# One load per expert tile, and the second layer's weights split a tile earlier

## The chip, the cores and the metric

One core of a Trainium2 chip runs the whole program. The metric is the device time of one execution in microseconds; the median of 3 runs stands for a kernel.

## The reference

Two transformer layers are computed in float32 for 2048 tokens of 512 features. The first has linear attention with 32 heads, and beside it a mixture of 16 experts, of which a router gives each token two; the second has softmax attention and 64 low-rank adapters. The part that matters here is the experts:

```python
def step(y, p):
    w1, b1, w2, b2, w3, b3, ge = p
    h = jax.nn.silu(xt @ w1 + b1) * (xt @ w2 + b2)
    return (y + ge[:, None] * (h @ w3 + b3), None)
```

w1 and w2 are 512x128 and w3 is 128x512 per expert; ge is the token's weight for the expert, zero for all but two of the 16.

## The kernel before

Ahead of the experts the kernel runs the first layer's attention, the router and a shared expert; that is most of the span. The tokens are sorted by expert into 31 tiles of 256 slots (`NTILES`, `SLOT_T`); a tile belongs to one expert, and slots that hold no token are skipped by the gather. `routed_experts` computes the tiles; the results go to `y_slots` in DRAM, from which the second layer collects them.

Every matrix product in float32 is made of three passes over pairs of a rounded "high" part and a "low" rest: high by high, high by low, low by high (`three_passes`). So each operand is split first: ScalarE rounds it (`eh`, `exth`, `ehh`), and another engine subtracts to get the rest (`el`, `extl`, `ehl`).

The work of tile i, by engine, in a software pipeline:

- SP loads the expert's weights: `load12` brings w1, w2 and the two biases (513 KB) into `raw12`, `load3` brings w3 (256 KB) into `raw3`; it stores the tile's output (`y_tiles`, 512 KB) and loads a piece of the second layer's weights (`load_piece`, 116 KB).
- GpSimd copies the tile's token numbers (`indices`), gathers the token rows in two halves of 128 into `xin` (`gather`, two indirect DMAs), splits a piece of the second layer's weights, and makes the low part of w3 (line 2263).
- TensorE transposes the token rows into PSUM (`rows_transposed`, line 2117), multiplies by w1 and w2 (`inner`) and by w3 (`outputs`).
- ScalarE rounds the transposed rows (line 2161), w3 (line 2166), copies the biases (2170), rounds w1 and w2 (2172), rounds the layer-1 piece (2176), computes the activation (2180), rounds its product (2182) and copies half of the output (2187).
- VectorE makes the low part of the rows (2195) and of w1 and w2 (2201), the product of the two branches (2213), its low part (2216), and copies the other half of the output (2221).

Each engine runs one function `run(r, b)` per step, in a loop over r with b = 0 and 1. `tile(r, b, ahead)` gives the tile that stands `ahead` tiles before the one whose outputs are made in that step. So in one step TensorE transposes tile s+2, multiplies tile s+1 by w1 and w2, and makes the outputs of tile s. ScalarE rounds the rows, w1 and w2 of tile s+2, and w3 of tile s+1; GpSimd gathers tile s+4 and makes the low part of w3 of tile s+1. SP loads w1 and w2 of tile s+4 and w3 of tile s+3.

All buffers are pairs, used by even and odd tiles. Engines wait on counts: `pe_xt` says that a tile's rows are transposed (its `xin` is free), `pe_o` that an output half is made (w3's `eh` and `el` of that tile are free), `v_lo` and `p_lo3` that the low parts of w1, w2 and of w3 are made (the raw buffers are free). Each engine's instructions are carried out in the order in which they are written; a wait holds up all that stands behind it on that engine.

Of the kernel before, what the change touches and what calls it, by code (L numbers as in the profile page):

```python
# [8 lines left out]
F32 = mybir.dt.float32  # L9
F32R = mybir.dt.float32r  # L10
I32 = mybir.dt.int32
ALU = mybir.AluOpType
ACT = mybir.ActivationFunctionType
AX_X = mybir.AxisListType.X

P = 128
# [12 lines left out]
SEC = KC * P  # L29
# [1954 lines left out]
def routed_experts(nc, new_sem, at, ps, ex, l1_w, xn_dram, y_slots, ident, expert_of, token_at, table_in, w1h, w1l,  # L1984
# [12 lines left out]
    def pair(name, shape, dt=F32):  # L1997
        return [sb(f"{name}{i}", shape, dt) for i in range(2)]

    def sem(name):  # L2000
        return new_sem("e_" + name)

    W12 = 2 * SEC + 2
    raw12, raw3 = pair("eraw12", [P, W12]), pair("eraw3", [P, SEC])
    xin, cur = pair("exin", [P, 2, D]), pair("ecur", [P, 2], I32)

    bias = pair("ebias", [P, 2])
    eh = pair("eh", [P, 3 * SEC], F32R)
    el, xth, xtl = ([sb(f"{n}0", [P, c], F32R)] for n, c in (("el", 3 * SEC), ("exth", KC * SLOT_T), ("extl", KC * SLOT_T)))
    assert end <= blocks_end  # L2010
    for some, n, c in ((el, "el", 3 * SEC), (xth, "exth", KC * SLOT_T), (xtl, "extl", KC * SLOT_T)):
# [3 lines left out]
    s1, hf = pair("es", [P, SLOT_T]), pair("ehf", [P, SLOT_T])  # L2015
    hh, hl = pair("ehh", [P, SLOT_T], F32R), pair("ehl", [P, SLOT_T], F32R)
    yb = pair("ey", [P, 2, D])
    banks = [b[:].rearrange("p (k s) -> p k s", k=2) for b in ps[0:6]]
    xt, hp, op = [banks[0:2], banks[2:4]], banks[4:6], ps[6:8]
    dma_w, dma_w3, dma_x, dma_y, dma_l1 = ([sem(f"{n}{i}") for i in range(2)]  # L2020
                                           for n in ("dma_w", "dma_w3", "dma_x", "dma_y", "dma_l1"))
    a_l1, lo_l1 = sem("a_l1"), sem("lo_l1")
    pe_xt, pe_h, pe_o, a_hi, a_hi3, a_xh, a_s, a_hh, a_y, v_lo, v_xl, v_hf, v_hl, v_y, p_lo3, p_cur, p_clear = (
        sem(n) for n in ("pe_xt", "pe_h", "pe_o", "a_hi", "a_hi3", "a_xh", "a_s", "a_hh", "a_y", "v_lo", "v_xl",
                         "v_hf", "v_hl", "v_y", "p_lo3", "p_cur", "p_clear"))
    y_tiles = y_slots.rearrange("(p i s) d -> i p s d", p=P, s=2)
    def w(j):
        return slice(j * SEC, (j + 1) * SEC)
# [13 lines left out]
    def tile(r, b, ahead, n=NTILES):  # L2042

        r, b = r + (b + ahead) // 2, (b + ahead) % 2
        i = r * 2 + b
        return not isinstance(i, int) or 0 <= i < n, i, r, b

    def wait(eng, sem_, n):

        if not isinstance(n, int) or n > 0:  # L2050
            eng.wait_ge(sem_, n)

    def sync(sp):
        def expert(i):
            return sp.value_load(expert_of[0:1, bass.ds(i, 1)], min_val=0, max_val=E - 1)

        def load12(i, b):
            e = expert(i)
            wait(sp, v_lo, i * 2 - 2)
            sp.dma_start(raw12[b][:], ex[e, :, 0:W12]).then_inc(dma_w[b], 16)  # L2060

        def load3(i, b):
            e = expert(i)
            wait(sp, p_lo3, i - 1)
            sp.dma_start(raw3[b][:], ex[e, :, W12:W12 + SEC]).then_inc(dma_w3[b], 16)

        def load_piece(i, b):
            if isinstance(i, int) and i == 0:
                sp.wait_ge(pe_xt, 4)
            wait(sp, lo_l1, i - 1)  # L2070
            sp.dma_start(l1raw[b][:], l1_w[:, bass.ds(i * PIECE, PIECE)]).then_inc(dma_l1[b], 16)

        def lead():
            blocks_used(sp)
            load12(0, 0)
            load3(0, 0)

        def run(r, b):
            is_tile, i, _, n = tile(r, b, 4)
            if is_tile:  # L2080
                load12(i, n)
            is_tile, i, _, n = tile(r, b, 3)
            if is_tile:
                load3(i, n)
            is_tile, i, _, n = tile(r, b, 0)
            if isinstance(i, int) and i == NTILES - LATE:

                for k in range(LATE):
                    c = slice(k * LATE_COLS, (k + 1) * LATE_COLS)
                    sp.dma_start(w1_late[:, c], l1_w[:, L_CUT + c.start:L_CUT + c.stop]).then_inc(dma_l1[0], 16)  # L2090
            if is_tile:
                sp.wait_ge(a_y, i + 1)
                sp.wait_ge(v_y, i + 1)
                sp.dma_start(y_tiles[i], yb[n][:]).then_inc(dma_y[n], 16)
            is_piece, i, _, n = tile(r, b, 2, PIECES)
            if is_piece:
                load_piece(i, n)

        def rest():
            load12(1, 1)  # L2100
            run(-1, 0)
            all_steps(sp, run)

        return lead, rest

    def tensor(pe):
# [47 lines left out]
    def scalar(a):  # L2154
        def run(r, b):
            is_tile, i, half, n = tile(r, b, 2)
            if is_tile:
                wait(a, pe_h, i - 1)
                for h in range(2):
                    a.wait_ge(pe_xt, i * 2 + h + 1)  # L2160
                    a.copy(xth[n][:, 2 * h:2 * h + 2, :], xt[n][h][:]).then_inc(a_xh, 1)  # L2161
            is_3, i3, half3, n3 = tile(r, b, 1)
            if is_3:
                wait(a, pe_o, i3 * 2 - 2)
                a.wait_ge(dma_w3[n3], half3 * 16 + 16)
                a.copy(eh[n3][:, w(2)], raw3[n3][:]).then_inc(a_hi3, 1)  # L2166
            if is_tile:
                a.wait_ge(dma_w[n], half * 16 + 16)
                wait(a, v_hf, i - 1)
                a.copy(bias[n][:], raw12[n][:, 2 * SEC:W12])  # L2170
                for j in range(2):
                    a.copy(eh[n][:, w(j)], raw12[n][:, w(j)]).then_inc(a_hi, 1)  # L2172
            is_piece, k, half_k, nk = tile(r, b, 0, PIECES)
            if is_piece:
                a.wait_ge(dma_l1[nk], half_k * 16 + 16)
                a.copy(w1h[:, bass.ds(k * PIECE, PIECE)], l1raw[nk][:]).then_inc(a_l1, 1)
            if is_3:
                a.wait_ge(pe_h, i3 + 1)
                wait(a, v_hf, i3 - 1)
                a.activation(s1[n3][:], hp[n3][:, 0, :], ACT.Silu, bias=bias[n3][:, 0:1]).then_inc(a_s, 1)  # L2180
                a.wait_ge(v_hf, i3 + 1)
                a.copy(hh[n3][:], hf[n3][:]).then_inc(a_hh, 1)
            is_tile, i, half, n = tile(r, b, 0)
            if is_tile:
                a.wait_ge(pe_o, i * 2 + 1)
                wait(a, dma_y[n], half * 16)
                a.copy(yb[n][:, 0, :], op[0][:]).then_inc(a_y, 1)

        return lambda: run(-1, 0), lambda: all_steps(a, run)

    def vector(v):
# [33 lines left out]
    def gpsimd(pool):  # L2225
        def indices(i, n):

            pool.wait_ge(table_in, 1)
            pool.tensor_copy(cur[n][:], token_at[:, bass.ds(i * 2, 2)]).then_inc(p_cur, 1)
            pool.wait_ge(p_cur, i + 1)  # L2230

        def gather(n):
            for s in range(2):
                pool.indirect_dma_start(xin[n][:, s, :], None, xn_dram,
                                        bass.IndirectOffsetOnAxis(ap=cur[n][:, s:s + 1], axis=0),
                                        bounds_check=T - 1, oob_is_err=False).then_inc(dma_x[n], 16)

        def lead():
            blocks_used(pool)
            for b in range(2):  # L2240
                pool.memset(xin[b][:], 0.0).then_inc(p_clear, 1)
            pool.wait_ge(p_clear, 2)
            for b in range(2):
                indices(b, b)
                gather(b)

        def run(r, b):
            is_tile, i, half, n = tile(r, b, 4)
            if is_tile:
                wait(pool, dma_x[n], half * 32)  # L2250
                indices(i, n)
                pool.wait_ge(pe_xt, i * 2 - 2)
            is_piece, k, _, nk = tile(r, b, -1, PIECES)
            if is_piece:
                c = bass.ds(k * PIECE, PIECE)
                pool.wait_ge(a_l1, k + 1)
                pool.tensor_tensor(w1l[:, c], l1raw[nk][:], w1h[:, c].bitcast(F32), ALU.subtract).then_inc(lo_l1, 1)
            if is_tile:
                gather(n)
            is_3, i3, _, n3 = tile(r, b, 1)  # L2260
            if is_3:
                pool.wait_ge(a_hi3, i3 + 1)
                pool.tensor_tensor(el[n3][:, w(2)], raw3[n3][:], eh[n3][:, w(2)].bitcast(F32),
                                   ALU.subtract).then_inc(p_lo3, 1)

        return lead, lambda: run(-1, 0), lambda: all_steps(pool, run)

    return {"sync": sync, "tensor": tensor, "scalar": scalar, "vector": vector, "gpsimd": gpsimd,
# [568 lines left out]
```

## Time and profile before

| what | us |
|---|---|
| median of 3 runs (2571.44 to 2572.82) | 2572.6 |
| the profiled execution | 2570.18 |
| its span | 2568.3 |
| TensorE busy in the span | 2495.5 |
| GpSimd busy | 1508.9 |
| VectorE busy | 1172.4 |
| ScalarE busy | 1152.2 |

Busy time of TensorE counts matmuls whose ends are modelled, so a busy TensorE need not be at its peak. The experts' stretch is about 180 us of the span, from 2066 to 2250 us. In rows of the trace, PE is TensorE, PEld its weight loads, DVE VectorE, ACT ScalarE, POOL GpSimd and SP the engine that issues loads and stores. `out<-in` names the tile written and those read, and what stands in square brackets is the idle time of the engine just before, with what ended it.

### The profile page before, as it was taken

What the parts mean: (1) busy time and instruction counts of PE and PEld (TensorE: products, weight loads), DVE (VectorE), ACT (ScalarE), POOL (GpSimd) and SP (SyncE); (2) the same over time, 40 slices, a digit from 0 to 9 for tenths busy, and PEclk for the clock granted to TensorE, in tenths of its full rate; (3) what the DMA queues carried; (4) which work ended last, traced back from release to release, by engine and by line L of the source; (5) the groups of instructions that cost most, each with busy time, mean ns of one, the idle gap of its engine ahead of it and who ended that gap; (6) DMA issues with size and microseconds to landing.
All of it is one profiled execution on the core that took longest, in us unless ns stands there. A gap on an engine that the chain in (4) does not pass through costs nothing.

```text
span 2568.3 us, 39435 instructions
## 1 busy us (share of the span) xinstructions
PE 2495.5 (97%) x13338; PEld 2140.1 (83%) x13338; DVE 1172.4 (46%) x1937; ACT 1152.2 (45%) x2182; POOL 1508.9 (59%) x1523
## 2 busy tenths in 40 slices
PE   7999999999999999999999999999999999969999
PEld 6888888888888888778888888888888888857777
DVE  6333333434343435763334343434343588865443
ACT  5444444444444444443444444444444457733332
POOL 5756656666575754765666766757575578731210
PEclk9999999999999999999999999999999999979999
DMA  4211110111111112211111011111111178931100
GB/s 166 87 48 40 55 63 31 63 47 61 36 58 47 56 40 99 94 48 48 40 55 63 31 63 47 59 35 61 47 56 40 60 245 305 301 101 34 37 29 33
DMA packets 84950, 188.00 MB, mean 73 GB/s; under 512 B 12610, under 2 KB 30674, under 8 KB 84870
## 3 DMA queue, kind: packets, MB, share of 16 engines
q1 hardware_dynamic: 76326, 170.13, 20.0%
q0 software_dynamic: 8544, 16.82, 2.2%
q8 instruction: 48, 0.79, 0.1%
q14 instruction: 32, 0.26, 0.0%
HBM read 168.00 MB, written 26.79 MB: 76 GB/s over the span
## 4 chain that ended last, share of the span: by engine, by line
PE 85%; DVE 7%; ACT 4%; issue 2%; DMA 1%; POOL 1%; ACTq 0%; SPq 0%; DVEq 0%
PE bank L95 24%; PE bank L96 23%; PE bank L97 23%; PE bank L1081 4%; PE bank L1064 4%; PE bank L1082 2%; PE bank L1065 2%; DVE el L2201 2%; ACT exth L2161 1%; ACT eh L2172 1%; ACT eh L2166 1%; DVE ehf L2213 0%; DMA l_stage<-y_slots,slot_of 0%; POOL l_stage L2720 0%; PE bank L539 0%
## 5 line engine op out<-in xcount | busy, mean ns | idle before, releaser
L1805 POOL TENSOR_TENSOR wl<-w_in,wh 128x512 fp32r<-128x512 f32 x510 | 587.7, 1179 | 189.5 <-ACT wh L1348 183.2
L95 PE MATMUL bank<-xh,wh 128*128 128x512 f32 x1400 | 560.7, 400 | 0.7 <-ACT bank L1296 0.7
L97 PE MATMUL bank<-xh,wl 128*128 128x512 f32 x1400 | 546.6, 390 | 0.0
L1823 POOL TENSOR_TENSOR sqacc<-sqacc,sq 128x512 f32<-128x512 f32 x128 | 165.6, 1294 | 379.3 <-ACT sq L1333 368.2
L1348 ACT CAST wh<-w_in 128x512 fp32r<-128x512 f32 x502 | 263.6, 567 | 274.0 <-POOL w_in L498 274.0
L96 PE MATMUL bank<-xl_sums,wh 128*128 128x512 f32 x800 | 315.8, 395 | 0.0
L97 PEld LDWEIGHTS bank<-xh,wl 128*128 128x128 f32 x1400 | 263.0, 188 | 57.3
L95 PEld LDWEIGHTS bank<-xh,wh 128*128 128x128 f32 x1400 | 263.5, 188 | 53.4 <-ACT bank L1296 0.9
L1602 DVE TENSOR_TENSOR acc<-bank,acc 128x512 f32<-128x512 f32 x240 | 165.7, 691 | 299.6 <-PE bank L97 299.6
L95 PE MATMUL bank<-wh,xh 128*128 128x256 f32 x912 | 260.3, 285 | 3.3 <-DVE xl L550 3.3
L96 PE MATMUL bank<-wl,xh 128*128 128x256 f32 x912 | 258.4, 283 | 0.0
L96 PE MATMUL bank<-xl,wh 128*128 128x512 f32 x600 | 234.6, 391 | 0.0
L1559 DVE TENSOR_TENSOR ms<-bank,dcur 128x384 f32<-128x384 f32 x256 | 142.3, 557 | 154.4 <-PE bank L1065 145.2
L95 PE MATMUL bank<-oh,yh 128*128 128x512 f32 x512 | 200.7, 392 | 6.7 <-DVE acc L1600 5.3
L1577 DVE SCALAR_TENSOR_TENSOR yf<-gT,bank 128x512 f32<-128x512 f32 x128 | 88.0, 687 | 249.1 <-PE bank L1082 249.1
L96 PE MATMUL bank<-ol,yh 128*128 128x512 f32 x512 | 200.0, 391 | 0.0
L97 PE MATMUL bank<-oh,yl 128*128 128x512 f32 x512 | 199.8, 390 | 0.0
L1582 DVE SCALAR_TENSOR_TENSOR yl<-yf,little,yh 128x512 fp32r<-128x512 f32 x128 | 131.0, 1023 | 137.0 <-ACT yh L1338 134.8
L1565 DVE TENSOR_TENSOR bank<-bank,t 128x512 f32<-128x512 f32 x128 | 89.5, 699 | 195.3 <-PE bank L97 183.5
L95 PEld LDWEIGHTS bank<-wh,xh 128*128 128x128 f32 x912 | 174.5, 191 | 4.9 <-DVE xl L550 2.1
L96 PEld LDWEIGHTS bank<-xl_sums,wh 128*128 128x128 f32 x800 | 150.6, 188 | 29.6
L96 PEld LDWEIGHTS bank<-wl,xh 128*128 128x128 f32 x912 | 174.5, 191 | 0.7
(354 smaller groups left out, 5394.4 us busy)
## 6 DMA issues: line engine op xcount, KB each, us to landing
w_in<-in_w_pairs_dram SPq DMA_DIRECT2D x100, 512.0 KB, 3.8
o_in<-in_o_pairs_dram SPq DMA_DIRECT2D x32, 512.0 KB, 4.8
eraw<-in_ex_dram SPq DMA_DIRECT2D x31, 513.0 KB, 5.1
y_slots<-ey SPq DMA_DIRECT2D x31, 512.0 KB, 6.0
w_in<-in_w_pairs_dram SPq DMA_DIRECT2D x56, 256.0 KB, 3.1
dcur<-in_decay_dram SPq DMA_DIRECT2D x32, 384.0 KB, 3.0
eraw<-in_ex_dram SPq DMA_DIRECT2D x31, 256.0 KB, 5.1
out_dram<-acc SPq DMA_DIRECT2D x16, 256.0 KB, 2.0
```

Of the source, the lines that this page charges most:

```text
L95: pe.matmul(out, wh, mh, start=start and i == 0, stop=False, skip_group_check=True)
L96: pe.matmul(out, wh, ml, start=False, stop=False, skip_group_check=True)
L97: ins = pe.matmul(out, wl, mh, start=False, stop=stop and i == n - 1, skip_group_check=True)
L1064: pe.matmul(sc[i % 2][:, 0:S], kT[:, hd, s0:s0 + P], qT[:, hd, s0:s0 + S], start=True, stop=True)
L1081: pe.matmul(out, v0, ms[i % 2][:, 0:S], start=True, stop=False, skip_group_check=True)
L1348: a.copy(wh[:, cols], w_in[:, cols]).then_inc(w_hi, 1)
L1559: v.tensor_tensor(ms[i % 2][:], sc[i % 2][:, 0:MC], dcur[:, ITEMS[i][0], :], ALU.mult).then_inc(v_mask, 1)
L1565: v.tensor_tensor(pj[2][:], pj[1][:], t5[:], ALU.add).then_inc(v_c, 1)
L1582: v.scalar_tensor_tensor(yl[g % 2][:], yf[:], nwcur[:, g % 2:g % 2 + 1], yh[g % 2][:].bitcast(F32), ALU.mult, ALU.subtract).then_inc(v_yl, 1)
L1602: v.tensor_tensor(now[:, t, :], op[t % 2][:], now[:, t, :], ALU.add).then_inc(v_acc, 1)
L1805: pool.tensor_tensor(wl[:, cols], w_in[:, cols], wh[:, cols].bitcast(F32), ALU.subtract).then_inc(w_lo, 1)
L1823: pool.tensor_tensor(sqacc[:, c], sqacc[:, c], sq[:], ALU.add).then_inc(p_sq, 1)
```

## The change

The two raw buffers become one of 1538 columns, with views `raw12` and `raw3` of it, and one load fills it. It waits for `p_lo3` alone. ScalarE rounds w3 of tile s+2 where it rounded that of tile s+1, and does it after the activation. GpSimd makes the low part of w3 of tile s+2 in a function `low3`, which also waits for `v_lo` of the same tile (so that `p_lo3` stands for the whole raw buffer), and which stands ahead of the gather in the step.

```diff
-    raw12, raw3 = pair("eraw12", [P, W12]), pair("eraw3", [P, SEC])
+    raw = pair("eraw", [P, W12 + SEC])
+    raw12, raw3 = [x[:, 0:W12] for x in raw], [x[:, W12:W12 + SEC] for x in raw]
...
-        def load12(i, b):
-            e = expert(i)
-            wait(sp, v_lo, i * 2 - 2)
-            sp.dma_start(raw12[b][:], ex[e, :, 0:W12]).then_inc(dma_w[b], 16)
-
-        def load3(i, b):
+        def load(i, b):
+
             e = expert(i)
             wait(sp, p_lo3, i - 1)
-            sp.dma_start(raw3[b][:], ex[e, :, W12:W12 + SEC]).then_inc(dma_w3[b], 16)
+            sp.dma_start(raw[b][:], ex[e]).then_inc(dma_w[b], 16)
...
             is_tile, i, _, n = tile(r, b, 4)
             if is_tile:
-                load12(i, n)
-            is_tile, i, _, n = tile(r, b, 3)
-            if is_tile:
-                load3(i, n)
+                load(i, n)
...
-            is_3, i3, half3, n3 = tile(r, b, 1)
-            if is_3:
-                wait(a, pe_o, i3 * 2 - 2)
-                a.wait_ge(dma_w3[n3], half3 * 16 + 16)
-                a.copy(eh[n3][:, w(2)], raw3[n3][:]).then_inc(a_hi3, 1)
...
+            is_1, i1, _, n1 = tile(r, b, 1)
+            if is_1:
+                a.wait_ge(pe_h, i1 + 1)
+                wait(a, v_hf, i1 - 1)
+                a.activation(s1[n1][:], hp[n1][:, 0, :], ACT.Silu, bias=bias[n1][:, 0:1]).then_inc(a_s, 1)
+            if is_tile:
+
+                wait(a, pe_o, i * 2 - 2)
+                a.copy(eh[n][:, w(2)], raw3[n]).then_inc(a_hi3, 1)
+            if is_1:
+                a.wait_ge(v_hf, i1 + 1)
+                a.copy(hh[n1][:], hf[n1][:]).then_inc(a_hh, 1)
...
+        def low3(i, n):
+
+            pool.wait_ge(a_hi3, i + 1)
+            pool.wait_ge(v_lo, i * 2 + 2)
+            pool.tensor_tensor(el[n][:, w(2)], raw3[n], eh[n][:, w(2)].bitcast(F32), ALU.subtract).then_inc(p_lo3, 1)
...
+            is_3, i3, _, n3 = tile(r, b, 2)
+            if is_3 and (b or not early):
+                low3(i3, n3)
             if is_tile:
                 gather(n)
-            is_3, i3, _, n3 = tile(r, b, 1)
-            if is_3:
-                pool.wait_ge(a_hi3, i3 + 1)
-                pool.tensor_tensor(el[n3][:, w(2)], raw3[n3][:], eh[n3][:, w(2)].bitcast(F32),
-                                   ALU.subtract).then_inc(p_lo3, 1)
```

GpSimd, one step of the loop before (`ecur` holds the token numbers, `exin` the gathered rows, `l_wl` the piece of layer 1, `el` and `eh` the low and high parts, `eraw` the raw weights):

```order
L2229 ISA [waits token_table_in,e_dma_x0]
L2229 COPY ecur_67<-token_at 128x2
L2230 REGISTER_ALU
L2252 REGISTER_ALU [waits e_p_cur]
L2256 ISA [waits e_pe_xt]
L2257 ISA [waits e_a_l1]
L2257 TENSOR_TENSOR l_wl<-l_raw_80,l_wh 128x232
L2234 DMA exin_65<-xn_rows,ecur_67 128x512 x2
L2262 ISA
L2263 TENSOR_TENSOR el_76<-eraw_64,eh_72 128x512 [waits e_a_hi3]
```

The same step on GpSimd in the change:

```order
L2222 ISA [waits token_table_in,e_dma_x0]
L2222 COPY ecur_65<-token_at 128x2
L2223 REGISTER_ALU
L2255 REGISTER_ALU [waits e_p_cur]
L2259 ISA [waits e_pe_xt]
L2260 ISA [waits e_a_l1]
L2260 TENSOR_TENSOR l_wl<-l_raw_78,l_wh 128x232
L2242 ISA
L2243 ISA [waits e_a_hi3]
L2244 TENSOR_TENSOR el_71<-eraw_61,eh_69 128x512 [waits e_v_lo]
L2227 DMA exin_63<-xn_rows,ecur_65 128x512 x2
```

The subtraction on w3 now stands ahead of the two gathers; it waits for one more signal, and it is that of the next tile (the other buffer of the pair, the one that the gather's tile will use).

ScalarE, one step of the loop before, from the second cast of the token rows on (`exth` rows, `ebias` biases, `es` activation, `ehh` the rounded product, `ey` output):

```order
L2161 CAST exth_77<-bank 128x512 [waits e_pe_xt]
L2051 REGISTER_ALU
L2166 CAST eh_71<-eraw_63 128x512 [waits e_dma_w30,e_pe_o]
L2170 COPY ebias_70<-eraw_62 128x2 [waits e_v_hf,e_dma_w1]
L2172 CAST eh_72<-eraw_62 128x512 x2
L2176 ISA [waits e_dma_l11]
L2176 COPY l_wh<-l_raw_80 128x232
L2180 ACTIVATE es_81<-bank,ebias_69 128x256 [waits e_v_hf,e_pe_h]
L2182 CAST ehh_85<-ehf_83 128x256 [waits e_v_hf]
L2185 REGISTER_ALU
L2187 COPY ey_90<-bank 128x512 [waits e_dma_y1,e_pe_o]
```

The same step on ScalarE in the change:

```order
L2153 CAST exth_75<-bank 128x512 [waits e_pe_xt]
L2157 COPY ebias_68<-eraw_62 128x2 [waits e_v_hf,e_dma_w1]
L2159 CAST eh_70<-eraw_62 128x512 x2
L2163 ISA [waits e_dma_l11]
L2163 COPY l_wh<-l_raw_78 128x232
L2168 ACTIVATE es_79<-bank,ebias_67 128x256 [waits e_v_hf,e_pe_h]
L2051 REGISTER_ALU
L2172 CAST eh_70<-eraw_62 128x512 [waits e_pe_o]
L2175 CAST ehh_83<-ehf_81 128x256 [waits e_v_hf]
L2178 ISA
L2180 COPY ey_88<-bank 128x512 [waits e_dma_y1,e_pe_o]
```

The cast of w3 has moved from behind the rows to behind the activation. It writes the buffer of the same tile as the casts of w1 and w2 ahead of it (70), where it wrote that of the tile before (71 beside 72).

## Rows read from the trace of the kernel before

**Rows 1.** The page: span, and slices of DMA share in tenths, 64 us each.

```profile
span 2568.3 us, 39435 instructions
...
DMA  4211110111111112211111011111111178931100
```

**Rows 2.** Stretches: from:to, length, busy us (count) of each engine, PEclk, DMA share, GB/s.

```profile
2072.00:2074.20 2.20, 0.17 (x1) 0.00 (x0) 2.20 (x5) 0.00 (x0) 0.47 (x1) 1.00 0.22 13
2075.10:2078.40 3.30, 3.30 (x18) 3.30 (x16) 2.81 (x5) 3.28 (x7) 2.33 (x3) 0.50 0.60 221
...
2083.00:2249.00 166.00, 157.79 (x1105) 140.26 (x1104) 141.16 (x204) 121.69 (x289) 129.76 (x137) 1.00 0.88 297
```

**Rows 3.** Waits, 2066 to 2250: who waits, for whom: us in all, times, longest.

```profile
DVE el L2201 <- ACT eh L2172: 9.7, 29, 0.5
...
PEld bank L95 <- DVE el L2201: 7.1, 17, 0.8
...
PE bank L2117 <- DMA exin<-xn_rows,ecur: 2.0, 4, 0.8
```

**Rows 4.** VectorE's timeline: start, us, engine, line, operation, count, idle before it.

```profile
2077.22 1.29 DVE L2201 TENSOR_TENSOR el<-eraw,eh 128x512 fp32r<-128x512 f32 x2 [0.38 <-ACT eh L2172]
...
2107.22 2.07 DVE L2201 TENSOR_TENSOR el<-eraw,eh 128x512 fp32r<-128x512 f32 x2 [0.33 <-ACT eh L2172]
...
2145.94 2.07 DVE L2201 TENSOR_TENSOR el<-eraw,eh 128x512 fp32r<-128x512 f32 x2 [0.33 <-ACT eh L2172]
...
2242.29 1.86 DVE L2201 TENSOR_TENSOR el<-eraw,eh 128x512 fp32r<-128x512 f32 x2 [0.33 <-ACT eh L2172]
```

**Rows 5.** ScalarE's timeline, one step of the loop.

```profile
2144.65 0.64 ACT L2166 CAST eh<-eraw 128x512 fp32r<-128x512 f32 x1
2145.17 0.21 ACT L2170 COPY ebias<-eraw 128x2 f32<-128x2 f32 x1
...
2146.88 0.47 ACT L2180 ACTIVATE es<-bank,ebias 128x256 f32<-128x256 f32 x1
2148.44 0.41 ACT L2182 CAST ehh<-ehf 128x256 fp32r<-128x256 f32 x1 [1.09 <-DVE ehf L2213]
```

**Rows 6.** TensorE's timeline, from one tile's transposes to the last output.

```profile
2140.78 1.04 PE L2117 MATMUL bank<-ident,exin 128*128 128x128 f32 x8
...
2146.82 1.09 PE L2117 MATMUL bank<-ident,exin 128*128 128x128 f32 x8 [0.34 <-DMA exin<-xn_rows,ecur]
...
2150.61 0.40 PE L95 MATMUL bank<-eh,ehh 128*128 128x512 f32 x1
...
2151.78 0.40 PE L97 MATMUL bank<-eh,ehl 128*128 128x512 f32 x1
```

**Rows 7.** GpSimd's timeline in the same step.

```profile
2143.18 1.04 POOL L2234 DMA_INDIRECT exin<-xn_rows,ecur  x1 [0.15 <-issue]
2144.53 1.00 POOL L2234 DMA_INDIRECT exin<-xn_rows,ecur  x1 [0.30 <-issue]
2145.56 1.29 POOL L2263 TENSOR_TENSOR el<-eraw,eh 128x512 fp32r<-128x512 f32 x1
```

**Rows 8.** DMA issues, 2090 to 2240: count, KB each, median us to landing.

```profile
eraw<-in_ex_dram SPq DMA_DIRECT2D x26, 513.0 KB, 5.1
...
eraw<-in_ex_dram SPq DMA_DIRECT2D x27, 256.0 KB, 5.2
...
exin<-xn_rows,ecur POOLq DMA_INDIRECT x50, 6.4
```

**Rows 9.** The tile exin: landings of its gathers.

```profile
DMA to landing us min/median/max: 2.1/6.2/8.1
```

**Rows 10.** DMA issues, 2077 to 2079: the pair of gathers at a nearly idle queue.

```profile
exin<-xn_rows,ecur POOLq DMA_INDIRECT x2, 3.0
```

**Rows 11.** DMA, 2154 to 2157: queue's packets, MB, share; and that step's gathers.

```profile
q1 hardware_dynamic: 259, 0.68, 70.4%
...
exin<-xn_rows,ecur POOLq DMA_INDIRECT x2, 4.6
```

More of the change, by code:

```diff
@@ L2019, in routed_experts @@
     xt, hp, op = [banks[0:2], banks[2:4]], banks[4:6], ps[6:8]
-    dma_w, dma_w3, dma_x, dma_y, dma_l1 = ([sem(f"{n}{i}") for i in range(2)]
-                                           for n in ("dma_w", "dma_w3", "dma_x", "dma_y", "dma_l1"))
+    dma_w, dma_x, dma_y, dma_l1 = ([sem(f"{n}{i}") for i in range(2)] for n in ("dma_w", "dma_x", "dma_y", "dma_l1"))
     a_l1, lo_l1 = sem("a_l1"), sem("lo_l1")
@@ L2074, in lead @@
             blocks_used(sp)
-            load12(0, 0)
-            load3(0, 0)
+            load(0, 0)
         def run(r, b):
@@ L2099, in rest @@
         def rest():
-            load12(1, 1)
+            load(1, 1)
             run(-1, 0)
@@ L2176, in run @@
                 a.copy(w1h[:, bass.ds(k * PIECE, PIECE)], l1raw[nk][:]).then_inc(a_l1, 1)
-            if is_3:
[L2178 to L2182, printed above, removed]
+            is_1, i1, _, n1 = tile(r, b, 1)
[9 more added lines that the diff above has]
+                a.copy(hh[n1][:], hf[n1][:]).then_inc(a_hh, 1)
             is_tile, i, half, n = tile(r, b, 0)
@@ L2245, in lead @@
                 gather(b)
+        def low3(i, n):
+            pool.wait_ge(a_hi3, i + 1)
+            pool.wait_ge(v_lo, i * 2 + 2)
+            pool.tensor_tensor(el[n][:, w(2)], raw3[n], eh[n][:, w(2)].bitcast(F32), ALU.subtract).then_inc(p_lo3, 1)
         def run(r, b):
+            early = isinstance(r, int) and r < 0
+            if early and b:
+                low3(0, 0)
             is_tile, i, half, n = tile(r, b, 4)
@@ L2257, in run @@
                 pool.tensor_tensor(w1l[:, c], l1raw[nk][:], w1h[:, c].bitcast(F32), ALU.subtract).then_inc(lo_l1, 1)
+            is_3, i3, _, n3 = tile(r, b, 2)
+            if is_3 and (b or not early):
+                low3(i3, n3)
             if is_tile:
                 gather(n)
-            is_3, i3, _, n3 = tile(r, b, 1)
-            if is_3:
-                pool.wait_ge(a_hi3, i3 + 1)
-                pool.tensor_tensor(el[n3][:, w(2)], raw3[n3][:], eh[n3][:, w(2)].bitcast(F32),
-                                   ALU.subtract).then_inc(p_lo3, 1)
         return lead, lambda: run(-1, 0), lambda: all_steps(pool, run)
```

## Prediction

> **What bounds the kernel now.** I read the page first for where the transfers are dense: the slices of DMA stand at 7, 8 and 9 in one short stretch after 2050 us [rows 1]. The span there belongs to the routed experts, the only part that the diff touches. The stretch view then says how it is filled: from 2083 to 2249 us TensorE is busy 157.79 of 166 us, no engine is free by much, and the DMA engines are busy 88% of the time [rows 2]. So a small shift can turn a hidden transfer into a wait. The view of waits names who is late for whom [rows 3]: VectorE waits for ScalarE's cast of the weights once in nearly every tile (29 times), TensorE waits for VectorE's subtraction, and four times TensorE waits for the gathered token rows.
>
> The timelines show the step of one tile. VectorE's subtraction of the first-layer weights starts at 2107.22 and, 24 tiles later, at 2242.29 [rows 4], so a step lasts 5.63 us on average. Two loops are close to that. ScalarE and VectorE feed each other: the cast L2166 of the second layer's weights stands between the casts of the tokens and of the first-layer weights [rows 5], and VectorE waits 0.33 us behind it [rows 4]. TensorE alone needs, from the start of a tile's transposes at 2146.82 to the end of the outputs at 2152.18 (2151.78 + 0.40), 5.36 us [rows 6]. Then the transposes of the next tile follow at once.
>
> The third loop matters most here. Let t be the tile that TensorE transposes at 2140.78. Its transposes free the buffer of token rows into which GpSimd gathers tile t+2. GpSimd starts the two halves of that gather at 2143.18 and 2144.53 [rows 7], so the second half is issued 3.75 us after the transposes began. It has until the transposes of t+2, two steps or 11.26 us after those of t. That leaves 7.5 us for landing. The median landing in the stretch is 6.4 us [rows 8], and all that the trace tells lie between 2.1 and 8.1 us [rows 9]: the cover is thin already, which is why TensorE waited for rows four times.
>
> **The change, part by part.**
>
> *One load instead of two.* SP issues one transfer of 769 KB per tile in place of 513 and 256 KB, and one read of the expert's number less. The bytes are the same. SP was not what anyone waited for; nothing is gained on the path. The load of tile t+2 now waits for low3(t), GpSimd's subtraction on the second layer's weights of tile t, instead of VectorE's. No row shows a 769 KB load; its landing lies between 5.1 us (the 513 KB piece alone) and 10.3 us (that and the 5.2 us of the other, one after the other) [rows 8]. I take 6.5, nearer the first, since both pieces overlap today. From its landing, ScalarE's bias and weight casts to the start of the activation take 1.71 us (2145.17 to 2146.88), then 0.47, the cast 0.64 and low3 1.29 [rows 5, 7]: 4.11 + 6.5 = 10.6 us for two steps, less than today's 11.26. The load stays hidden. The store of the outputs and the load of a layer-1 piece stand behind the load on SP; both have two buffers, so a delay of some us is covered.
>
> *The cast one tile sooner.* On ScalarE the cast for tile t now stands after the activation and waits until TensorE has finished the outputs of tile t-2, since they read the same buffer. The place that it leaves is worth 0.52 us (2144.65 to 2145.17) in the loop of ScalarE and VectorE [rows 5], and the new place is one where ScalarE idled 1.09 us for VectorE. Also low3 no longer runs beside VectorE's pair of subtractions, which took 2.07 us beside it and 1.29 without [rows 4]. Alone, these would take that loop below TensorE's 5.36 us.
>
> *The gather behind low3.* This is the term that decides. GpSimd's queue is in order, and low3(t) now stands ahead of the gather of t+2. Low3(t) waits for ScalarE's cast, which waits for the outputs of t-2. On TensorE these come after the transposes of t and the products of t-1. So from the start of the transposes of t: 5.36 us to the end of those outputs [rows 6], 0.64 us cast [rows 5], 1.29 us low3, 1.35 us from the first to the second half of the gather (2143.18 to 2144.53) [rows 7]. The second half is issued at 8.64 us, where it was 3.75. Then it must land before the transposes of t+2. Two steps last 8.64 us plus the landing L, if that exceeds 2 x 5.36. Break-even with today's 11.26 is L = 2.6 us.
>
> What L will be: the bounds are 3.0 us, the median of the pair that met a nearly idle queue at 2077 [rows 10], and 6.4, that of the crowded stretch [rows 8]. With longer steps the DMA share falls to about 0.88 x 5.63 / 6.8 = 0.73. The pair at 2154 to 2157 met such a queue (SP's transfers took 70% of the engines' time) and landed in 4.6 us [rows 11], though hardly any bytes were gathered there; and the new load of 769 KB is released at the same moment as the gather. I take L = 5.0. Two steps are then 13.64 us, one is 6.82, or 1.19 us more than now. The gathers of tiles 3 to 30 stand behind a low3: 28 x 1.19 = 33.3 us.
>
> The Trainium skill (DMA: Bandwidth & Descriptors, Anatomy of one DMA) puts a transfer at about 2.0 us plus its bytes over 436 GB/s; for a full half of 256 KB I estimate 2.6 us from it, by which two steps would be 11.24 us and the change would cost nothing. Here the trace disagrees: 6.4 us is the median with other transfers in flight [rows 8], and the page's figure is for one by itself.
>
> *TensorE's clock.* With L = 5.0 TensorE waits 13.64 - 10.72 = 2.92 us in every two tiles. In the trace before, a wait of about 2 us (0.17 us busy from 2072.0 to 2074.2) was followed by 3.30 us at a granted clock of 0.50, the lower of the two levels (1.2 GHz) [rows 2]; work that would take 1.65 us at 2.4 GHz took 3.30. Whether the new wait stands in one piece or is spread over the two tiles the trace can't say. Bounds: no fall, 0 us; one in each of 14 pairs, 23 us. I take three, 5 us, as the waits divide unevenly with the number of rows gathered.
>
> *What queues behind the new wait.* On ScalarE, the cast of the activations to tile t-1's outputs: 0.64 + 0.41 on ScalarE [rows 5] and one subtraction on VectorE, needed 3.79 us after the next transposes start (2146.82 to 2150.61) [rows 6]; covered. On GpSimd only the gather, which is the term above.
>
> **Sum.** 33.3 + 5 = 38.3 us. The profiled execution took 2570.18 us, 1.9 above its span of 2568.3 [rows 1] and 2.4 below the median of 2572.6. Against the median: 2572.6 + 38.3, about 2611 us.
>
> **The rivals.**
>
> *Faster.* If the gather lands within 2 x 5.36 - 8.64 = 2.08 us of its second issue, the new order costs nothing, the loop of ScalarE and VectorE is relieved, and TensorE's 5.36 us binds: 28 x 0.27 = 7.6 us less, 2565 us. For it: the relief is real by the rows. Against it: the least landing seen is 2.1 [rows 9]. Chance 0.05.
>
> *No difference.* A gather that lands in about 2.6 us leaves 2573 us; that is the case of a transfer by itself. Landings of 3 us and less occur only when the queue is nearly empty [rows 10], which a released load of 769 KB prevents. The Trainium skill's page on DMA, above, would have it so. Chance 0.06.
>
> *A mild loss.* L = 3.5 to 4.2, because the gathers of half-empty tiles carry few bytes: steps of 6.1 to 6.4 us, 12 to 22 us more, 2585 to 2595 us. Chance 0.17.
>
> *A fall of the clock in every pair.* 33.3 + 23 = 56 us, 2629 us; with L = 6.4 as well, 53 + 23, 2649 us. For it: the wait of 2.92 us exceeds the one that did it at 2074. Against it: in the present stretch TensorE waits a little in many tiles [rows 3] and the clock stays at 1.00 [rows 2]. Chance 0.14.
>
> **How the numbers follow.** The forecast (L = 4.4 to 5.8, at most a few falls) has 0.58. The low end of the range lies just under the mild loss, 2584; the high end takes in most of the falling clock, 2642. A measurement of this kernel tells about 0.2% (5 us) from no change. Faster by more than that 0.05, within it 0.06, slower 0.89.
>
> **What would show it.** Right: the period of VectorE's subtraction rises to 6.5 to 7.2 us; TensorE's longest wait in the stretch is for the gathered rows and comes to 25 us or more in total, where it was 2.0; GpSimd waits for the cast of the second layer's weights in each tile; the cast starts within some tenths of the end of the outputs; the DMA share falls to about 0.73; VectorE's pair takes some 1.3 us. Wrong: TensorE's wait for rows stays small, or the second half of the gather is issued less than 7 us after the transposes began, or it lands in under 3 us.

## The result and the profile after

The change takes 2644.22 us (median of 4 runs, 2640.42 to 2646.99) against 2572.1 us: 72 us more, a ratio of 1.0283 with a 95% interval of 1.027 to 1.0296. The forecast was slower, 2611 us, with a range that ended at 2642 us. The direction and the place were right, the size was not.

The page of the kernel after, its span, the granted clock of TensorE and the DMA share in slices of 66 us:

```profile
span 2638.6 us, 39227 instructions
...
PEclk9999999999999999999999999999999988889999
DMA  4211111111111113111111111111110666721110
```

The span was 2568.3 us and the DMA slices stood at 7, 8 and 9 [rows 1]. Now the stretch is longer and emptier, and the clock stands at 8 tenths in slices of it where it was at 9 or more.

VectorE's timeline gives the step (start, us, operation, idle before): its subtraction of the first-layer weights starts at 2106.16 and 24 tiles later at 2304.34.

```profile
2106.16 1.30 DVE L2194 TENSOR_TENSOR el<-eraw,eh 128x512 fp32r<-128x512 f32 x2
...
2161.44 1.21 DVE L2209 TENSOR_TENSOR ehl<-ehf,ehh 128x256 fp32r<-128x256 f32 x1 [1.27 <-ACT ehh L2175]
...
2304.34 1.29 DVE L2194 TENSOR_TENSOR el<-eraw,eh 128x512 fp32r<-128x512 f32 x2
```

That is 8.26 us a tile; it was 5.63 [rows 4]. 28 tiles at 2.63 us more are 74 us: the whole loss lies in the steps. The pair of subtractions takes 1.29 us, as foretold. The row between, the subtraction of the activations' product, takes 1.21 us; it took 0.43 before, of which more below.

The view of waits, from 2066 to 2320 us (who waits for whom, us in all, times, longest):

```profile
POOL el L2244 <- ACT eh L2172: 88.2, 29, 9.4
...
PE bank L2109 <- DMA exin<-xn_rows,ecur: 62.4, 21, 5.6
...
ACT eh L2172 <- PE bank L97: 25.7, 29, 0.9
```

TensorE waits 62.4 us for gathered rows, where it was 2.0 [rows 3]. Behind that stand the two waits that the change adds: GpSimd for the cast of w3 in almost every tile, and ScalarE, ahead of that cast, for TensorE's outputs.

One turn of the loop (from the transposes of a tile to those two tiles later) can be followed in the timelines. TensorE begins the transposes of a tile, call it t, at 2143.34. The last of the outputs of t-2 is issued at 2148.25 and ends at 2148.65, 5.31 us later; [rows 6] gave 5.36.

```profile
2143.34 1.03 PE L2109 MATMUL bank<-ident,exin 128*128 128x128 f32 x8
...
2148.25 0.40 PE L97 MATMUL bank<-eh,ehl 128*128 128x512 f32 x1
2153.51 1.91 PE L2109 MATMUL bank<-ident,exin 128*128 128x128 f32 x8 [4.87 <-DMA exin<-xn_rows,ecur]
```

ScalarE's cast of w3 for t waits for those outputs and starts as they end:

```profile
2148.68 0.62 ACT L2172 CAST eh<-eraw 128x512 fp32r<-128x512 f32 x1 [0.93 <-PE bank L97]
```

GpSimd makes the low part at 2149.47 and only then issues the two halves of the gather of t+2, at 2150.71 and 2152.06. The last row is of the next turn:

```profile
2146.92 1.00 POOL L2227 DMA_INDIRECT exin<-xn_rows,ecur  x1 [0.30 <-issue]
...
2149.47 1.09 POOL L2244 TENSOR_TENSOR el<-eraw,eh 128x512 fp32r<-128x512 f32 x1 [0.23 <-ACT eh L2172]
2150.71 1.05 POOL L2227 DMA_INDIRECT exin<-xn_rows,ecur  x1
2152.06 1.00 POOL L2227 DMA_INDIRECT exin<-xn_rows,ecur  x1 [0.30 <-issue]
...
2163.87 1.01 POOL L2227 DMA_INDIRECT exin<-xn_rows,ecur  x1 [0.30 <-issue]
```

SP issues the load of 769 KB between these two halves, and the output's store behind it:

```profile
2151.05 0.35 SPq L2061 DMA_DIRECT2D eraw<-in_ex_dram  x1
2151.72 0.35 SPq L2086 DMA_DIRECT2D y_slots<-ey  x1
```

The second half is issued 8.72 us after the transposes of t, where 8.64 was worked out. What follows wasn't foreseen. The second half of the other gather in these rows, that of t+1, was issued at 2146.92, and TensorE's transposes waited for it until 2153.51: 6.59 us, of which the chain below counts 6.31 as its landing, and TensorE stood still for 4.87 of them. And the turn that begins with these late transposes is longer: its second half is issued at 2163.87, 10.36 us after 2153.51.

The chain of waits, five of its longest pieces in a row (start, us, what), shows such a landing once in every two tiles:

```profile
2113.04 6.54 DMA exin<-xn_rows,ecur
2129.95 6.52 DMA exin<-xn_rows,ecur
2146.92 6.31 DMA exin<-xn_rows,ecur
2163.87 5.87 DMA exin<-xn_rows,ecur
2180.17 6.46 DMA exin<-xn_rows,ecur
```

From 2095 to 2300 the landings on the chain lie between 5.8 and 7.3 us, 6.4 at the median. The pieces start 16.3 to 17.0 us apart: a landing, and 10.4 to 10.6 us from its end to the next issue.

The stretch view (from:to, length, busy us and count of TensorE, its weight loads, VectorE, ScalarE, GpSimd; granted clock, DMA share, GB/s) for the experts, and then for one wait and what follows it:

```profile
2083.00:2300.00 217.00, 155.62 (x997) 140.48 (x995) 127.86 (x188) 115.69 (x266) 111.19 (x137) 0.91 0.69 208
2148.70:2153.50 4.80, 0.00 (x0) 0.00 (x0) 2.20 (x3) 1.39 (x3) 3.68 (x4) 1.00 1.01 352
2153.60:2157.00 3.40, 3.40 (x17) 3.40 (x18) 1.61 (x3) 2.13 (x5) 0.80 (x2) 0.50 0.87 271
2157.10:2160.00 2.90, 2.90 (x22) 2.71 (x21) 1.20 (x3) 0.83 (x3) 0.00 (x0) 1.00 0.31 107
```

During the wait TensorE does nothing and the DMA engines are full (1.01, 352 GB/s). Then the clock is at 0.50, the lower of its two levels, for 3.4 us of work. Then the DMA engines stand at 0.31. Over the stretch the DMA share is 0.69 and the clock 0.91, where they were 0.88 and 1.00 [rows 2]. The turn at 2153.51 is 1.64 us longer than that at 2143.34, about what 3.4 us at half the clock lose: the fall comes right behind the wait, inside the loop. So in this turn the engines, evenly busy before, alternate: the transfers are released together, and TensorE waits for them.

### The profile page after: what moved, and what is told of

It is laid out like the page before. It is cut to its first block, busy times and chain, and to the rows that moved or that the text cites. A ratio compares the mean times of both kernels' runs of the same rounds, so it can differ in the third digit from the quotient of the medians.

```text
span 2638.6 us, 39227 instructions
## 1 busy us (share of the span) xinstructions
PE 2507.0 (95%) x13338; PEld 2152.6 (82%) x13338; DVE 1170.6 (44%) x1937; ACT 1156.9 (44%) x2182; POOL 1493.8 (57%) x1523
## 4 chain that ended last, share of the span: by engine, by line
PE 86%; DVE 5%; DMA 4%; ACT 2%; issue 2%; POOL 1%; POOLq 0%; SPq 0%; DVEq 0%; ACTq 0%
PE bank L95 24%; PE bank L96 24%; PE bank L97 24%; PE bank L1081 4%; PE bank L1064 4%; DMA exin<-xn_rows,ecur 3%; PE bank L1082 2%; PE bank L1065 2%; PE bank L2109 1%; DMA l_stage<-y_slots,slot_of 0%; POOL l_stage L2721 0%; DVE xl L550 0%; ACT eh L2172 0%; PE bank L2486 0%; PE bank L539 0%
```

## The experiments

Two theories stood against each other. G: the gather behind low3, behind the cast, behind the outputs, closes a loop over two tiles. W: the single load that waits for low3 is what comes late. Times are medians; ratios are against the kernel before on the same chip.

**The gather first.** Only the order within GpSimd's step is undone.

```diff
+            if is_tile:
+                gather(n)
             is_3, i3, _, n3 = tile(r, b, 2)
             if is_3 and (b or not early):
                 low3(i3, n3)
-            if is_tile:
-                gather(n)
```

> The change, but in GpSimd's step the gather of tile t+2 stands ahead of low3(t) again. Theory G (the gather behind low3, cast and outputs closes a loop of 8.64 us plus its landing over two tiles): the loop opens, 2560 to 2578 us, TensorE's waits for gathered rows under 8 us in all. Theory W (the single load that waits for low3 is what comes late): stays above 2620 us, with ScalarE waiting for the weights.

Measured: 2576.9 us, ratio 1.0019 (1.001 to 1.0029). Of the 72 us, 67 are gone by two lines moved. Theory W is refuted as the main cause. But the version doesn't gain, and TensorE still waits for rows, 14.0 us against the 8 expected at most. Its waits, and its stretch from 2083 to 2250:

```profile
POOL el L2244 <- ACT eh L2172: 19.7, 13, 4.5
ACT l_wh L2163 <- DMA l_raw<-in_l_w_dram: 19.0, 15, 2.9
...
PE bank L2109 <- DMA exin<-xn_rows,ecur: 14.0, 13, 1.8
```

```profile
2083.00:2250.00 167.00, 152.69 (x1103) 138.46 (x1102) 133.43 (x203) 124.84 (x287) 123.04 (x137) 1.00 0.91 295
```

One wait has grown from 1.8 us in the kernel before: that of ScalarE for the piece of layer 1, whose load stands behind the weights' load on SP. The DMA engines are at 0.91.

**The kernel before with low3 first.** The same order in the kernel before, and nothing else.

```diff
+            is_3, i3, _, n3 = tile(r, b, 1)
+            if is_3:
+                pool.wait_ge(a_hi3, i3 + 1)
+                pool.tensor_tensor(el[n3][:, w(2)], raw3[n3][:], eh[n3][:, w(2)].bitcast(F32),
+                                   ALU.subtract).then_inc(p_lo3, 1)
             if is_tile:
                 gather(n)
-            is_3, i3, _, n3 = tile(r, b, 1)
...
```

> The kernel before, with the low part of w3 ahead of the gather in GpSimd's step and nothing else. Low3 there waits for a cast that ended at 2145.29 in the trace before, so the gather would start about 3.4 us later: second half issued near 7.1 us after the transposes, and two steps of 13.5 us with a landing of 6.4. Theory G: 2587 to 2617 us. Theory W, or a theory that the cast one tile sooner is what costs: within 5 us of the kernel before.

Measured: 2578.57 us, ratio 1.0027 (1.0015 to 1.0038). It costs about 7 us (by the interval 4 to 10): below all that G gave, and over the 5 us of the other theories, though not clear of it. TensorE's wait for rows rose, but to 16 us only, and GpSimd's timeline shows why:

```profile
PE bank L2117 <- DMA exin<-xn_rows,ecur: 16.2, 13, 2.1
```

```profile
2148.64 1.29 POOL L2261 TENSOR_TENSOR el<-eraw,eh 128x512 fp32r<-128x512 f32 x1
2150.09 1.31 POOL L2234 DMA_INDIRECT exin<-xn_rows,ecur  x1 [0.15 <-issue]
2151.70 1.00 POOL L2234 DMA_INDIRECT exin<-xn_rows,ecur  x1 [0.31 <-issue]
...
2154.26 0.68 POOL L2257 TENSOR_TENSOR l_wl<-l_raw,l_wh 128x232 f32 x1 [1.18 <-PE bank L2117]
2155.21 1.31 POOL L2261 TENSOR_TENSOR el<-eraw,eh 128x512 fp32r<-128x512 f32 x1 [0.27 <-ACT eh L2166]
```

Low3 waits 0.27 us or nothing for the cast in these rows, and never more than 0.35 us from 2089 to 2237. The second half of the gather goes out 5.8 us after the transposes began (2145.92 to 2151.70), not the 7.1 that I had expected. That cast stands early in ScalarE's step and doesn't wait for the outputs just made; I had taken its end from a trace in which nothing hurried it. So the order alone is cheap. It becomes dear when low3 waits for a cast that waits for TensorE.

**A small load.** It separates the landing's two parts, the gather's own time and the crowd.

```diff
-            sp.dma_start(raw[b][:], ex[e]).then_inc(dma_w[b], 16)
+            cols = slice(0, W12 + SEC if isinstance(i, int) and i < 2 else 64)
+            sp.dma_start(raw[b][:, cols], ex[e, :, cols]).then_inc(dma_w[b], 16)
```

> The change, with the weights' load of tiles 2 to 30 cut to 64 of 1538 columns (32 KB); the rest of the weights stays that of tiles 0 and 1. Theory G with the landing made long by the load released beside it: landing 3 to 4.5 us, steps near 6.3 us, few falls of the clock, 2580 to 2605 us. G with a landing that is the gather's own: 2632 to 2650 us. Theory W: back to 2565 to 2577 us.

Measured: 2605.48 us, ratio 1.0127 (1.011 to 1.0144), half a us above what G gave. Pieces of its chain, and its stretch from 2083 to 2280:

```profile
2126.85 4.58 DMA exin<-xn_rows,ecur
...
2141.78 4.56 DMA exin<-xn_rows,ecur
...
2160.51 4.61 DMA exin<-xn_rows,ecur
```

```profile
2083.00:2280.00 197.00, 162.83 (x1076) 149.06 (x1075) 133.42 (x198) 122.44 (x285) 115.49 (x140) 0.91 0.44 140
```

The landing on the chain is mostly 4.6 us where it was 6.4 at the median: some 2 us of it is the weights' load released at the same moment. The clock still falls (0.91), which I hadn't reckoned with.

**TensorE kept busy.** It prices the clock.

```diff
+            if not isinstance(i, int) or i >= 4:
+                pe.wait_ge(v_xl, i * 2 - 3)
+                for _ in range(14):
+                    pe.transpose(xt[n][0][:, 0, 0:P], ident[:], ident[:])
             pe.wait_ge(dma_x[n], half * 32 + 32)
```

> The change, with 14 more transposes of the identity (about 1.8 us) on TensorE ahead of each wait for gathered rows, from tile 4 on. The clock fell 13 times in windows of 3.41 us in the experts' stretch after the change; if each costs up to 1.65 us, and work in the wait keeps the clock up: 2618 to 2632 us, granted clock near 1.00 in the stretch. If the falls are hidden in the wait and cost nothing: within 5 us of the change, 2639 to 2650 us.

Measured: 2624.3 us, ratio 1.0208 (1.0191 to 1.0225). More work on TensorE makes the program 20 us shorter. The stretch from 2083 to 2280:

```profile
2083.00:2280.00 197.00, 177.56 (x1339) 164.51 (x1339) 131.65 (x186) 115.35 (x264) 108.19 (x132) 0.99 0.73 223
```

The granted clock is 0.99 instead of 0.91. Half of the time at the lower level is lost: at a mean of 0.91 over 217 us that is 0.09 x 217 = 20 us, which is what came back.

**Small load and busy TensorE together** (the small load's diff, and 8 transposes instead of 14).

> The change with the weights' load of tiles 2 to 30 cut to 32 KB, and with 8 more transposes of the identity (1 us) on TensorE ahead of each wait for rows, from tile 4 on. It takes the clock out of the small load's time. If the small load's steps are (8.77 + L)/2 with the L of about 4.5 that its trace shows, 6.6 us a tile: 2590 to 2600 us, with few or no windows of lower clock. If the falls of the clock cost nothing there: 2600 to 2608 us.

Measured: 2598.22 us, ratio 1.0099 (1.0083 to 1.0114). The clock is at 1.00 in the stretch from 2083 to 2260, and the landing on the chain again 4.5 to 4.8 us:

```profile
2083.00:2260.00 177.00, 162.49 (x1222) 150.95 (x1222) 132.19 (x190) 116.06 (x270) 112.78 (x136) 1.00 0.45 141
```

```profile
2136.79 4.57 DMA exin<-xn_rows,ecur
...
2156.72 4.66 DMA exin<-xn_rows,ecur
```

With 4.6 us, the loop gives (8.64 + 4.6) / 2 = 6.6 us a tile, 28 x 0.99 = 28 us more than before; measured were 27. Against the small load alone only 7 us came back (2605.48 to 2598.22), although that stretch stood at 0.91 too and the sum made for the busy TensorE would give 0.09 x 197 = 18 us. So that sum is no fixed price of a fall; why less came back here was not shown.

**One load, alone.** The kernel before with its loads joined and the rest of it as it was; the load of tile s+3 is issued where that of w3 was.

```diff
+            is_tile, i, _, n = tile(r, b, 3)
+            if is_tile and not (isinstance(i, int) and i < 2):
+                load(i, n)
...
                 pool.wait_ge(a_hi3, i3 + 1)
+                pool.wait_ge(v_lo, i3 * 2 + 2)
```

> The kernel before with its two loads made one and nothing else of the change: the load of tile s+3 waits for low3 of tile s+1, the cast stays a tile later, the gather stays first. From the rows before: landing 5.2 to 6 us, then 5.65 us on ScalarE from the bias to the end of the next cast of w3 and 1.29 us low3 make a loop of 12.1 to 12.9 us over two tiles, 6.1 to 6.5 us a tile: 2585 to 2597 us if the single load needs the cast a tile sooner; within 5 us of the kernel before if the single load costs nothing by itself.

Measured: 2587.84 us, ratio 1.0061 (1.0044 to 1.0077), as expected. Its waits:

```profile
DVE el L2193 <- ACT eh L2164: 44.4, 27, 4.2
ACT ebias L2162 <- DMA eraw<-in_ex_dram: 33.7, 18, 3.8
...
PE bank L95 <- DVE el L2193: 20.1, 13, 3.2
```

ScalarE waits for the weights, and VectorE and TensorE behind it. So joining the loads does need the cast a tile sooner; it is the price of one signal for a buffer that three subtractions read.

**What remains when the gather is first.** Three versions ask why moving the gather back didn't also bring the gain of the relieved loop. First, two loads again (gather first, cast a tile sooner):

```diff
         def load(i, b):
             e = expert(i)
-            wait(sp, p_lo3, i - 1)
-            sp.dma_start(raw[b][:], ex[e]).then_inc(dma_w[b], 16)
+            wait(sp, v_lo, i * 2 - 2)
+            sp.dma_start(raw12[b], ex[e, :, 0:W12]).then_inc(dma_w[b], 16)
...
+        def load3(i, b):
+            e = expert(i)
+            wait(sp, p_lo3, i - 1)
+            sp.dma_start(raw3[b], ex[e, :, W12:W12 + SEC]).then_inc(dma_w3[b], 16)
```

> The change with the gather ahead of low3, and with two loads again: w1, w2 and the biases wait for VectorE's signal as in the kernel before, w3 for low3, issued behind the output's store. What is left of the change is the cast of w3 one tile sooner. Theory S (with the gather in front, the single load that waits for low3 is what still costs, 5 us): 2558 to 2570 us. Theory D (the DMA engines, 0.91 busy in the stretch, take what ScalarE's and VectorE's loop gives): 2570 to 2578 us.

Measured: 2569.16 us, ratio 0.9991 (0.9982 to 1.0001): in the range of S, though not clear of no change.

Second, the single load, with the cast of the layer-1 piece behind that of the activations' product on ScalarE:

```diff
-            is_piece, k, half_k, nk = tile(r, b, 0, PIECES)
-            if is_piece:
-                a.wait_ge(dma_l1[nk], half_k * 16 + 16)
-                a.copy(w1h[:, bass.ds(k * PIECE, PIECE)], l1raw[nk][:]).then_inc(a_l1, 1)
...
                 a.copy(hh[n1][:], hf[n1][:]).then_inc(a_hh, 1)
+            is_piece, k, half_k, nk = tile(r, b, 0, PIECES)
+            if is_piece:
+                a.wait_ge(dma_l1[nk], half_k * 16 + 16)
+                a.copy(w1h[:, bass.ds(k * PIECE, PIECE)], l1raw[nk][:]).then_inc(a_l1, 1)
```

> The change with the gather ahead of low3, and with ScalarE's cast of the layer-1 piece moved from ahead of the activation to ahead of its output copy. In the run with the gather first ScalarE waited 19.0 us for that piece, and the activation stood behind it. Theory Q (that wait is what keeps the version from gaining): 2558 to 2569 us. Theory D: 2570 to 2580 us, with the wait moved to the gathered rows or the weights.

Measured: 2572.05 us, ratio 1.0001 (0.9992 to 1.0011): in D's range; against the run with the piece ahead the ratio fell by 0.0018, some 5 us, with intervals that just touch. TensorE's wait for rows fell from 14.0 to 10.1 us, and ScalarE's wait for the weights rose from 9.6 to 12.1.

Third, both:

> Both of the last two edits together: gather first, two loads, the layer-1 piece cast late. Theories Q and S: 2555 to 2566 us, TensorE's 5.36 us a tile as the bound. Theory D: 2568 to 2576 us.

Measured: 2567.85 us, ratio 0.9989 (0.9979 to 1.0), between the two ranges, so it was measured again:

> The version with the gather first, two loads and the layer-1 piece cast late, again, with more rounds, against the kernel before. Its first runs gave a ratio of 0.9989. Expected 0.998 to 0.9995 if its steps of 5.51 us are real (28 x 0.13 = 3.6 us less than the kernel before); 1.000 if that was chance.

Measured: 2567.31 us, ratio 0.9985 (0.9976 to 0.9994). This version beats both kernels, by 4 us over the one before, just clear of noise. Of the change it holds one part alone, w3 split a tile sooner, with the low part behind the gather; the later cast of the piece is an edit of its own. Its wait for rows and its stretch from 2083 to 2235:

```profile
PE bank L2119 <- DMA exin<-xn_rows,ecur: 4.9, 7, 1.2
```

```profile
2083.00:2235.00 152.00, 146.35 (x1067) 134.18 (x1065) 132.50 (x197) 119.69 (x280) 119.95 (x135) 1.00 0.91 308
```

## Why the prediction was right or wrong

**Right: where it is lost.** The period rose by a wait of TensorE for gathered rows, GpSimd waits for the cast in 29 of 31 tiles, the cast starts as the outputs end, the DMA share fell (0.69; 0.73 was said), VectorE's pair takes 1.29 us. At the full clock the second half of a gather is issued as late as worked out (8.72 us against 8.64). Moving the gather back took 67 of the 72 us away. The load stayed hidden, as said: a 769 KB load landed in 5.2 us, near my lower bound; the output's store took 6.9 us, and no wait for it shows.

```profile
eraw<-in_ex_dram SPq DMA_DIRECT2D x24, 769.0 KB, 5.2
y_slots<-ey SPq DMA_DIRECT2D x24, 512.0 KB, 6.9
```

**Wrong: the landing, "I take L = 5.0".** It is 6.4 on the chain at the median. Together with the falls of the clock it brings the period to 8.26 us, outside the 6.5 to 7.2 that I had named as a sign of being right. I let L fall with the mean DMA share, from 0.88 to some 0.73. The share did fall, but the landing didn't, since low3 releases the gather and the load of 769 KB at the same moment, and the output's store goes out with them: during TensorE's wait the DMA engines are at 1.01, and afterwards at 0.31. I named that load as a reason to go above 4.6, and went 0.4 us above; cutting it took 1.8 us off. What makes the other 4.6 us, against the 3.0 of [rows 10], was not tried; the store of 512 KB is still in it. Nor was the late cast with low3 first and two loads, so what the order costs without the joined load is open.

**Wrong: "I take three", the falls of the clock.** In the turn followed above the price was right (1.64 us); the count was too low. At 0.91 over 217 us, the lower level holds 0.18 x 217 = 39 us, 11 to 12 falls as long as the 3.3 us of [rows 2], in place of three. The waits are not spread: in the turn above one tile waits 4.87 us and its neighbour none, and 4.87 us is more than twice the wait that brought the clock down at 2074. 20 us were lost where I gave 5.

Put together: with a landing of 6.4 the prediction's own sum gives (8.64 + 6.4) / 2 = 7.52 us a tile, 28 x 1.89 = 53 us. The version with TensorE kept busy, whose landing on the chain is 6.3 at the median, lost 53 (2624.3 against 2571.22). The clock is the other 20: 73 against the 72 measured. How much of this is the load beside the gather depends on what is taken away first: the small load gave back 26 us with TensorE kept busy (2624.3 to 2598.22, with 14 and 8 transposes), and 39 without (2644.22 to 2605.48).

The rival with a fall of the clock in every pair, 2629 to 2649 us, held the result, and had a chance of 0.14. Its two conditions were not independent, as I had treated them: the crowd lengthens the wait, and with the longer wait the clock fell more often.

**Half right, and of little weight here: the gain on ScalarE and VectorE.** VectorE's pair did fall from 2.07 to 1.29 us. But low3 now runs beside the subtraction of the activations' product, which rose from 0.43 to 1.21: the 0.78 us were moved, not won, and VectorE's busy time over the span is 1170.6 us where it was 1172.4. The prediction didn't ask beside what low3 would run instead. Of the gain worked out, the place on ScalarE is left. Two loads, the gather first and the piece late give 4 us of the 7.6 that I worked out for that case. Whether the DMA engines, at about 0.9 in that stretch, keep the rest was not shown.

## What to carry to other kernels

On an in-order queue, ask of each instruction moved ahead of a DMA issue what its slowest wait waits for: one that reaches back to the engine that the DMA feeds closes a loop, and the landing is then paid every turn. Joining two loads under one signal can make transfers leave together, as here, so take the landing from the moment when all of them are in flight, not from a mean share. A wait on TensorE of several us has to be priced with the fall of the clock behind it; a little idle work in the wait gave back 20 us here. And when an instruction stops running beside another, ask beside which one it runs now.

## What the runs showed of the hardware

The subtraction of the activations' product on VectorE (128x256, both inputs in SBUF) took 1.21 us at 2161.44 in the kernel after, when GpSimd's low3 had started 0.17 us before it; it took 0.43 us in the kernel before, where low3 ran elsewhere:

```profile
2143.35 0.43 DVE L2216 TENSOR_TENSOR ehl<-ehf,ehh 128x256 fp32r<-128x256 f32 x1 [0.47 <-ACT ehh L2182]
```

```profile
2161.27 1.10 POOL L2244 TENSOR_TENSOR el<-eraw,eh 128x512 fp32r<-128x512 f32 x1 [4.88 <-ACT eh L2172]
```

In the kernel before, low3 stood beside VectorE's pair, which took 2.07 us instead of 1.29 [rows 4]. Both times low3 had started first, and VectorE's work took 0.78 us longer. The Trainium skill (SBUF — State Buffer, Who interferes with whom) says that a VectorE instruction with two SBUF inputs contends with a GpSimd instruction that reads SBUF. The trace agrees, with these 0.78 us. Low3 itself took 1.10 us, where it was 1.29 [rows 7]. VectorE's product of the two branches, which reads PSUM for one of its inputs, took its usual 0.47 us at 2148.62 beside GpSimd's subtraction on the layer-1 piece (2148.53 to 2149.24).
